# A decoder layer on one Trainium2 core: the first shared expert moved beside the end of the cross attention, blank rows and routed weights written and loaded earlier

## What is computed

```python
x = _layernorm(x + _L0_attn_ref(x, ...))               # gated delta rule, short and long filters, a gate over 5 paths
x = _layernorm(x + _L0_xattn_ref(x, ctx_1024, ...))    # cross attention, 16 heads of 16
x = _layernorm(x + _L0_ffn_ref(x, ...))                # 2 shared experts and 8 routed ones, F = 352

def _swiglu(x, wg, wu, wd):
    return jax.nn.silu(x @ wg) * (x @ wu) @ wd
...
for i in range(sh_gate.shape[0]):
    shared = shared + _swiglu(x, sh_gate[i], sh_up[i], sh_down[i])
w, sel = jax.lax.top_k(probs, K)                       # K = 2 of the 8 for each token
...
for e in range(exp_gate.shape[0]):
    routed = routed + Wte[:, e:e + 1] * _swiglu(x, exp_gate[e], exp_up[e], exp_down[e])
out = shared + SCALE * routed
```

## Time and profile before

| what | value |
|---|---|
| time, median of 3 runs | 1064.91 us (1063.68 to 1065.12) |
| the profiled execution's own time | 1069.18 us |
| its span | 1067.1 us |
| instructions | 18321 |
| PE busy | 887.9 us (83%) |
| DVE busy | 627.0 us (59%) |
| ACT busy | 424.3 us (40%) |
| POOL busy | 353.6 us (33%) |
| moved by DMA | 103.78 MB |
| mean granted clock of TensorE | 0.923 of full speed |

### The profile page before, as it was taken

One profiled execution on the slowest core, in us unless ns is written; L12 is line 12 of the kernel. 1 busy time (PEld: TensorE's weight loads), 2 busy tenths in 40 slices (PEclk: granted clock), 3 DMA queues, 4 the chain that ended last, 5 costly groups with the idle time before them and its releaser, 6 DMA issues. The chain is left out here.

```text
span 1067.1 us, 18321 instructions
## 1 busy us (share of the span) xinstructions
PE 887.9 (83%) x6859; PEld 659.5 (62%) x6859; DVE 627.0 (59%) x1458; ACT 424.3 (40%) x747; POOL 353.6 (33%) x327
## 2 busy tenths in 40 slices
PE   6788677779889897898788888775497999999796
PEld 5566555656667665686455555443386677777675
DVE  4788797366998988544456667653322243333155
ACT  5677544355555544442233344332131232222221
POOL 9322200023446555324000222223343142222395
PEclk9899988879998987999789999997599999999898
DMA  5689469976454431121000000000371222221321
GB/s 161 197 234 280 136 98 213 324 152 153 100 110 105 75 70 50 49 80 51 1 11 6 27 30 31 21 21 21 124 261 49 83 60 62 69 60 55 108 90 60
DMA packets 141287, 103.78 MB, mean 97 GB/s; under 512 B 90704, under 2 KB 127632, under 8 KB 140304
## 3 DMA queue, kind: packets, MB, share of 16 engines
q1 hardware_dynamic: 137408, 92.17, 33.2%
q0 software_dynamic: 3792, 10.44, 2.6%
HBM read 71.33 MB, written 31.25 MB: 96 GB/s over the span
## 5 line engine op out<-in xcount | busy, mean ns | idle before, releaser
L1887 ACT ACTIVATE pT<-ps 128x2048 f32<-128x2048 f32 x32 | 60.0, 1874 | 126.7 <-PE ps L1864 126.7
L2348 PE MATMUL ps<-wr,xbT 128*128 x312 | 101.4, 468 | 1.9 <-ACT xbT L2384 1.9
L1840 DVE TENSOR_REDUCE mx<-ps 128x8 f32<-128x2048 f32 x32 | 73.4, 2293 | 48.1 <-PE ps L1819 48.1
L2437 POOL DMA_INDIRECT y_dram<-yb,dest_row x39 | 37.8, 968 | 137.8 <-DVE dest_row L2413 133.6
L2348 PEld LDWEIGHTS ps<-wr,xbT 128*128 128x128 f32 x312 | 59.8, 193 | 30.6 <-issue 4.3
L1259 POOL TENSOR_TENSOR st<-st,exponent 128x20 f32<-128x20 f32 x16 | 56.5, 3534 | 65.8 <-DVE st L1234 64.5
L526 DVE SCALAR_TENSOR_TENSOR room<-room 128x256 f32<-128x256 f32 x144 | 58.3, 480 | 15.3 <-ACT room L476 15.3
L642 PE MATMUL ps<-hank,win 128*32 128x192 f32 x512 | 45.1, 515 | 19.4 <-DVE room L560 9.0
L1819 PE MATMUL ps<-kept,cq 32*128 32x256 f32 x512 | 38.6, 418 | 22.5 <-ACT pT L1887 19.5
L2363 PE MATMUL ps<-wdr,hbT 128*128 (+1 forms) x234 | 56.9, 379 | 0.0
L2422 DVE TENSOR_TENSOR hb<-bsg,ps 128x352 f32<-128x352 f32 x39 | 20.3, 521 | 61.1 <-PE ps L2348 61.1
(11 more groups left out here) (355 smaller groups left out, 2272.7 us busy)
## 6 DMA issues: line engine op xcount, KB each, us to landing
room<-in_gW SPq DMA_DIRECT2D x8, 1280.0 KB, 7.4
tok_dram<-room SPq DMA_DIRECT2D x8, 768.0 KB, 5.0
fir_dram<-room SPq DMA_DIRECT2D x6, 1024.0 KB, 8.3
paths<-fir_dram SPq DMA_DIRECT2D x48, 128.0 KB, 3.7
xb<-xs_dram SPq DMA_DIRECT2D x39, 130.0 KB, 2.4
yr<-y_dram SPq DMA_DIRECT2D x16, 256.0 KB, 3.9
delta_room<-tok_dram SPq DMA_DIRECT2D x4, 768.0 KB, 6.8
kept<-tok_dram SPq DMA_DIRECT2D x4, 768.0 KB, 5.6
```

Source lines behind the costliest of these rows:

```text
L1840: V.tensor_reduce(mx[:, :, g, XD:P:CH].rearrange("p t c -> p c t"), ps[:, 0:NCH, :].rearrange("p c (t k) -> p c t k", t=TT), AX.X, ALU.max ...
L1887: S.activation(pT[g % 2][:].rearrange("p c k t -> p (c k t)"), ps[:, 0:NCH, :].rearrange("p c n -> p (c n)"), ACT.Exp).then_inc(*s.ex.up())
L2348: m = nc.tensor.matmul(ps[:, 2 * (j % 2) + half, 0:FF], xbT[j % 2][:, k, :], wr[:, bass.ds(e, 1), k, half, :].rearrange("p e n -> p (e n)" ...
```

## The change

Six things are changed together.

1. Shared expert 0 becomes a class `Shared` whose engine parts are generators; its 14 units are put beside steps 10 and 11 of the cross attention, ten in step 10 and four in step 11. `free` has every engine wait until the attention's buffers, whose room the expert uses now, are no longer read; `tokens` waits for the tokens of a group. The expert's meeting of its own is gone.
2. The down results of expert 0 go through bank 4 alone, so a pair must be read before the next is written.
3. The block table is put beside step 11: six steps before DVE's last pair of additions, twelve behind it.
4. Blank rows: ACT fills all of `xs_dram` with four DMAs in step 8 of the delta phase, each of 32 partitions, with one row read 137 times from each partition. POOL's first row store waits for them. The eight indirect stores and SP's one are gone.
5. The routed weights: `wr` is loaded before steps 1 to 8 of the cross attention, `wdr` (three tensors now, in rooms that are free by then) before step 10.
6. Rooms: the attention's buffers and the expert's share `cross_room`; the value buffers are two instead of three, and POOL fills them one step later.

```diff
+    env.blank = sb("blank", [P, XW])
...
+        def act_blank():
+
+            act.wait_ge(kv.blank, 2)
+            places = env.xs_dram.rearrange("(p n) w -> p n w", p=P)
+            for k in range(4):
+                q = slice(k * CH, (k + 1) * CH)
+                nc.scalar.dma_start(places[q], env.blank[q].unsqueeze(1).broadcast_to([CH, (NE * STRIDE + P) // P, XW])).then_inc(
+                    *kv.blank_out.up(16))
...
-        weave([act_invert, act_states, act_statistics, act_gate, act_project_out], B, {2: act_parameters}, act_beside)
+        weave([act_invert, act_states, act_statistics, act_gate, act_project_out], B, {2: act_parameters, 8: act_blank}, act_beside)
...
-        def pool_queries(b):
-            pool.wait_ge(s.pv_made, XG * (b - 2))
+        def pool_values(b):
+            pool.wait_ge(s.pv_made, XG * (b - 1))
...
+            pool.wait_ge(env.kv.blank_out, 64)
             pool.wait_ge(s.route, 11 * b + 11)
...
-        pg.meet(rows_out)
+        def sp_routed_up(e):
+            for j, n in enumerate(("exp_gate", "exp_up")):
+                nc.sync.dma_start(env.wr[:, e, :, j], a[n][e].rearrange("(k p) n -> p k n", p=P)).then_inc(*experts.routed_in.up(16))
...
+        def sp_last():
+
+            sp.wait_ge(s.pv_made, XG * B)
+            sp.wait_ge(s.ex, XG * B)
+            sp.wait_ge(s.mx_turned, 2 * B)
+            sp_routed_down(0)
+            sp_routed_down(1)
+            copied(sp, "y", B - 1)
+            sp_routed_down(2)
...
+        def free(eng):
+            eng.wait_ge(s.pv_made, XG * B)
+            eng.wait_ge(s.ex, XG * B)
+            eng.wait_ge(s.oT, 2 * B)
+
+        def tokens(eng, tg):
+
+            eng.wait_ge(s.kept, 2 * (tg + 1))
+            eng.wait_ge(s.lo, 2 * (tg + 1))
+
+        def beside(units, tables=None):
+            return {B + 2: some(units, B + 2), B + 3: units if tables is None else both(units, tables)}
+
+        def both(units, tables):
+
+            for n, _ in enumerate(units):
+                if n >= 2:
+                    next(tables, STOP)
+                yield
+            for _ in tables:
+                pass
...
+        weave([pe_queries, pe_maxes, pe_attend, pe_output, pe_place], B, {B + 2: lambda: free(pe)}, beside(firsts.pe(tokens)))
...
+        weave([dve_queries, dve_maxes, dve_attend, dve_output, dve_place], B, {B + 2: lambda: free(dve)},
+              beside(firsts.dve(tokens), dve_table()))
...
+        pg.meet([*rows_out, experts.routed_in])
...
-        for e in range(NE):
-            G.indirect_dma_start(env.xs_dram, bass.IndirectOffsetOnAxis(ap=spare[:, e:e + 1], axis=0), blank[:],
-                                 None).then_inc(*spare_out.up(16))
...
+        tg, half = down
+        bank = 4 if self.e == 0 else 4 + 2 * (tg % 2) + half
+        return tg, half, (self.e * NG_X + tg) * 2 + half, bank, 1 if self.e == 0 else 4
...
-                pe.wait_ge(s.acc, 2 * (d - 4) + 2)
+                pe.wait_ge(s.acc, 2 * (d - others) + 2)
```

More of the change, by code:

```diff
@@ L137, in weave, with some @@
         interleave(parts + [beside[s]] if s in beside else parts)
+def some(pieces, n):
+    for _ in range(n):
+        next(pieces, STOP)
+        yield
 def idle(b):
@@ new lines, in phase_cross, with sp_weights @@
+        dve_table = place_tokens(pg, env, experts)
+        def sp_weights(e):
+            if e == 0:
+                sp_shared_weights(pg, a, env, 0)
+            sp_routed_up(e)
+        sp_before = {e + 1: lambda e=e: sp_weights(e) for e in range(NE)} | {B + 2: sp_last}
+        weave([sp_queries, idle, idle, idle, idle], B, sp_before)
+        weave([pe_queries, pe_maxes, pe_attend, pe_output, pe_place], B, {B + 2: lambda: free(pe)}, beside(firsts.pe(tokens)))
+        weave([act_queries, idle, act_attend, act_output, idle], B,
+              {1: lambda: act_shared_weights(pg, env, 0), B + 2: lambda: free(act)}, beside(firsts.act()))
@@ new lines, in phase_cross, with place_tokens, take, table @@
+        weave([dve_queries, dve_maxes, dve_attend, dve_output, dve_place], B, {B + 2: lambda: free(dve)},
+              beside(firsts.dve(tokens), dve_table()))
+        weave([idle, pool_values, idle, pool_output, pool_place], B,
+              {1: lambda: pool_shared_weights(pg, env, 0), B + 2: lambda: free(pool)}, beside(firsts.pool()))
+        pg.meet([*rows_out, experts.routed_in])
+    pg.leave(s)
+def place_tokens(pg, env, s):
+    V, dve = pg.nc.vector, pg.dve
+    n_t, at = NTOK // P, [0]
+    def take(size, pattern="p n -> p n", **sizes):
+        at[0] += size
+        return views(env.tables, at[0] - size, size, pattern, **sizes)
+    count, limit, blocks, ended = take(NE), take(n_t), take(NE), take(NE)
+    first_f, least = take(NB), take(NB)
+    last = at[0]
+    past = take(NB * NE, "p (b e) -> p b e", e=NE)
+    at[0] = last
+    over, upto = take(NE * n_t, "p (e n) -> p e n", e=NE), take(NE * NE, "p (e f) -> p e f", e=NE)
+    def table():
+        full, no = env.filled[:, 0], env.expert_no
@@ new lines, in table, with before, units, __init__ @@
+        step(V.tensor_tensor(env.spill, env.spill, env.row_no[:, 0:1].broadcast_to([P, NB]), ALU.add))
+        yield
+    return table
+NG_X, NFT = NTOK // TG, len(FT)
+def before(q):
+    return q - (1, 3, 2)[q % NFT]
+def units():
+    for tg in range(NG_X + 1):
+        for n in range(NFT):
+            up, down = tg < NG_X, tg > 0 and n > 0
+            if up or down:
+                yield (tg, n) if up else None, (tg - 1, n - 1) if down else None
+class Shared:
+    def __init__(self, pg, env, s, e):
+        self.pg, self.env, self.s, self.e = pg, env, s, e
+    def unit(self, up):
+        tg, n = up
+        return tg, n, *FT[n], n % 2, (self.e * NG_X + tg) * NFT + n
+    def result(self, down):
+        tg, half = down
+        bank = 4 if self.e == 0 else 4 + 2 * (tg % 2) + half
+        return tg, half, (self.e * NG_X + tg) * 2 + half, bank, 1 if self.e == 0 else 4
+    def pe(self, tokens=None):
+        nc, pe, env, s, e = self.pg.nc, self.pg.pe, self.env, self.s, self.e
+        ps, w, wd, sw = env.ps, env.w, env.wd, env.weights
@@ L2449, in phase_experts, with all_units @@
+            if at:
+                at(k, down)
+            yield
+def all_units(program):
+    for _ in program:
+        pass
+def phase_experts(pg, a, env):
+    nc, pe, act, dve, pool, sp = pg.nc, pg.pe, pg.act, pg.dve, pg.pool, pg.sp
+    V, S, G = nc.vector, nc.scalar, nc.gpsimd
+    s, y_out = env.experts, [pg.unused() for _ in range(4)]
+    ps, ident, acc, wr, wdr = env.ps, env.ident, env.x2, env.wr, env.wdr
+    out = a["out"].rearrange("b (t p) d -> p (b t) d", p=P)
     with ExitStack() as inner:
@@ new lines, in phase_experts, with sp_blocks @@
+        dest_row = sb("dest_row", [P, NI], U32)
+        x_in = [*s.x_in0, *s.x_in1]
+        pg.meet([])
+        def sp_blocks():
+            for j in range(NB):
+                if j == 2:
+                    sp_shared_weights(pg, a, env, 1)
+                sp.wait_ge(s.xT_made, j - 3)
+                sp.wait_ge(s.info, 4 * (j - 3))
+                row = nc.sync.value_load(env.first_row[0:1, j:j + 1], min_val=0, max_val=NE * STRIDE)
+                nc.sync.dma_start(xb[j % 4][:], env.xs_dram[bass.ds(row, P)]).then_inc(*x_in[j % 4].up(16))
```

497 lines of the change are left out of this document (221 added, 276 removed).

## The result

The changed kernel takes 1123.03 us (median of 4 runs, 1115.95 to 1128.14) against 1065.01 us before: a ratio of 1.0542, 95% interval 1.048 to 1.0603. It is slower by 58 us. The forecast was slower at 1103 us, with a range that ended at 1114, so the direction held and the size did not.

A forecast was written before the change was run, and what follows sets the result against it. PE, busy 83% of the span, was taken as the bound, with holes in the last two cross-attention steps. 1069.2 − 17 (weave) + 55 (ACT held) = 1107.2; this execution lay 4.3 above the median, so 1103 us, range 1049 to 1114.

The forecast's parts named there:

- Part 3: Four blank DMAs on ACT in the delta phase: ACT held in its issues until 12.0 MB are gone, 55 us lost.
- The other reading, room for 2,550 in all: Blank DMAs: rings hold 2,550 rows in all, so ACT is held 72 to 101 us; 1120 to 1149 us, chance 0.05.
- Both rivals that had ACT free or at full rate: Blank DMAs: ACT not held, 1054 us, chance 0.34; or held 30 us at full rate, 1077 us, chance 0.18.
- the line that I drew over the doublings: Blank DMAs' rate from 32 partitions, interpolated between 150 and 395 GB/s: about 230, taken as 210.
- Loss 55 us.: Delta phase: ACT held 57 us from 382.4 to 439.4 instead of going on at 384.22; ahead-work and slow clock cancel.
- rival 1: Blank DMAs: ACT not held, later context loads about 3 us late once or twice; 1054 us, 1048 to 1062, chance 0.34.
- the 70 to 76 named as its sign: Weave: 70 to 76 us from step 10 to the first block's load, PE over 85% busy, clock near full.
- The expert's 55.3: Weave: PE's time in shared expert 0, 765.61 to 820.9, kept unchanged in the 66.2 us sum.
- The nine handovers at 0.33: Weave: waits left at the cross attention's small groups, some nine at 0.33 us, 3.0 us in all.
- The bank's wait: Weave: PE waits for DVE to read the shared result bank, 1.1 us once, at the last token group.
- The tail: Behind the weave's last product: DVE's pair 0.3 + 0.76, table steps, 1.2 for the meeting; 799.5 to 805.6.
- the 22 given as the bound: Weave's gain, priced at 17 us: 22 if the small groups' waits stay hidden and the table costs half.

## Why the prediction was right or wrong

**Right: the side and ACT's hold.** Part 3 read in three issue rows of weight loads that an engine is held in its issue when some 1,600 pieces stand ahead. It was so: counted from the packets that had begun to move, 1,536, 1,569 and 1,441 stood ahead at the ends of ACT's second to fourth issue. The list of DMA queues from 386 to 450.17, the end of the fourth issue, has 11,711 of the 13,152 ahead of it gone:

```profile
q10 hardware_dynamic: 11711, 12.15, 96.3%
```

(By 186 rows/us from the end of the first issue they come to 1,390 for the second and 1,340 for the fourth; the rows began to move 0.7 us later. The pieces of 3,120 bytes had 1,192 to 1,299 ahead.) The other reading, room for 2,550 in all, is out (81 us where 74.92 were measured for eight DMAs). Both rivals that had ACT free or at full rate did not come.

**Wrong size, term one: the rate.** The forecast put 210 GB/s for 32 partitions; the trace shows 194, and ACT's hold, 63.5 us instead of 57, cost 61.4 instead of 55. The Trainium skill, page "SBUF — State Buffer", section "Door 1: The DMA port swizzle", gives 189 GB/s for partitions 0 to 31, in transfers of 1 MiB. The trace's 194 agree with it, for each of the four groups of 32 partitions, and the prediction's 63 us from it were nearer than the line that I drew over the doublings.

**Wrong, term two: the path through SP was left out.** The step that failed is that the loss ends when ACT comes free ("to 439.4", "**Loss 55 us.**"). The loads of paths stood in the sum only as something that shares the DMA engines with the rows and so lowers their rate to 210. That the rows lengthen those loads, and that PE waits for `dx_gate` behind them, was put at nothing. When ACT came free some 5,800 rows had still to go. SP stood 28.20 us in its six loads instead of 4.38, since their 6,144 short pieces took turns with the rows, and PE waited 12.86 us for `dx_gate`. Later loads stood in rival 1 alone, and there at the context loads; in fact those were not the ones that came late, since the rows had drained by then. Without these 13 us the time would have been 1110, inside the range. A simple reckoning: SP's six loads and the drain of all 18.24 MB, 94 us at 194 GB/s, end together, so PE's two waits come to the drain less the work done between.

**Wrong size, term three: the weave gained 24.7, not 17.** From step 10 to the first block's load are 64.86 us, under the 70 to 76 named as its sign. PE needed 59 us from step 10 to its last product, where the sum had 66.2. The expert's 55.3 had in it the slow clock of its first 4 us and 1.8 us of waiting, which the weave takes away; without them it is 144 × 0.233 + 144 × 0.12 = 51, from the pitch of its products in the changed kernel (12 in each of 12 up parts, and 18, not 24, in each of 8 down parts). The nine handovers at 0.33 were not there: behind the first (0.22) no small group waited, as each has products of the expert ahead of it. The bank's wait was 1.8 us in two pieces instead of 1.1 in one. The tail was right: 5.8 us from the end of the last product to the block's load, with 3.7 of table and 1.2 for the meeting in it, where the sum had 6.1. 24.7 is beyond the 22 given as the bound.

**Right: what was costed at nothing.** Weights that are loaded earlier, the third value buffer, ACT's two table loads, POOL's tail: none shows in a wait of PE in the stretch.

The two errors of the loss (6 and 13) and the one of the gain (8, the other way) leave 12 us. The other 8 of the 20 between forecast and result are 2 in stretches that the change does not touch, and 6 between the profiled executions, 51.9 apart, and the medians, 58 apart. On another chip the medians were 48 apart, so those 8 are no error of a term.

## What to carry to other kernels

Before a large DMA is put on an engine's queue, count its pieces, not its bytes: an issue that costs 0.7 us on an empty queue costs the whole drain of what exceeds some 1,400 pieces ahead of it on its engine's queue. Then ask what the other engines load meanwhile, and in what pieces: their pieces take turns with those of the large DMA, so loads in many short ones (1,024 of 128 bytes here) suffer most, and whatever is queued behind them comes late. An issue of few pieces goes through, but its data land late (10.2 us here instead of 2.3). Cut such a transfer into parts that drain within one step, spread them over steps that are really that long, let each read all partitions, and look at the issue rows of all engines, which are not counted as busy. And when two stretches are woven, price PE by its products' pitch at full clock, not by its time in the old stretch, in which the slow clock of a restart is hidden.

## What the runs showed of the hardware

- Four DMAs of 4,384 rows of 1,040 bytes held their engine 0.70, 16.06, 23.46 and 23.90 us; eight of 2,192 rows held it 74.92 in all, and pieces of 3,120 bytes were counted like those of 1,040.
- An issue was accepted with 1,441 to 1,569 pieces of 1,040 bytes ahead on ACT's queue, 1,192 to 1,299 of 3,120 bytes, and 1,384 to 1,538 on SP's, counted apart: SP's went through while 4,864 of ACT's stood queued.
- The DMA engines took pieces of both queues in turn, 2,928 of ACT's and 2,978 of SP's in 16 us, whatever their length. SP stood 28.20, 20.37 and 19.19 us in six loads of 1,024 pieces each that take it 4.4 alone.
- What SP issued began to move 6.9 to 7.0 us later, behind 1,275 to 1,296 of ACT's rows at 194 GB/s, and 4.4 us later, behind 1,242, at 296.
- The rate of these writes was 194 GB/s from 32 partitions (204 in pieces three times as long) and 296 from 128, each at a DMA share of 0.98 to 1.10, so the share tells that the engines are taken, not how much they move.
